# Attention block: 24 of 36 probability tiles turned through memory in the second batch, one fetch a tile, y kept in the order of rows 4 i + a

## The chip, the cores and the metric

One NeuronCore of a Trainium2 chip runs one program. Its engines are TensorE (PE, matmuls; its weight loads are PEld), VectorE (DVE), ScalarE (ACT), GpSimd (POOL) and SyncE (SP, which here only issues DMAs). ACT issues DMAs too, on a queue of its own. The metric is the device time of one execution in microseconds (us), the median of the runs; lower is better.

## The reference, cut to what matters

```python
x = x + attention(layernorm(x))        # x: 2 batches x 1024 rows x 512
x = x + lora_mixture(layernorm(x))

def attention(x):                      # 32 query heads, 8 key/value heads, head size 128
    q, k, v = x @ Wq.T, x @ Wk.T, x @ Wv.T          # split into heads
    q, k = rmsnorm(q) * q_norm_w, rmsnorm(k) * k_norm_w
    scores = q @ k.T / sqrt(128) + slope[head] * (column - row)     # causal
    return softmax(scores) @ v @ Wo.T

def lora_mixture(x):                   # 8 experts of rank 16
    gates = 8 * softmax(x @ Wr.T + br)
    return 2 * sum over experts of gates * ((x @ A.T) @ B.T)
```

All values are float32. Softmax, the products and both sums have to come out in float32 precision, so the kernel splits the operand of a large product into a high and a low part and multiplies three times.

## The kernel before

**Work and stages.** `attention_lora_block` goes through 16 groups, numbered w = 0 to 15. A group is one key/value head with its G = 4 query heads in one batch; w = 0 to 7 are the first batch, 8 to 15 the second. Within a group it goes through s = 0 to 7, the row tiles of P = 128 query rows. The first batch turns and splits the weights on the chip and keeps the results in memory (`keep_wkv`, `keep_wq`, `keep_wo`); the second batch loads them back (`back_wkv`, `back_wq`, `back_wo`). The second half of the block (the items that begin with `f_`, and `logits`, `lora`) runs for the first batch in groups 7 and 8 and for the second in group 15.

**One row tile.** `scores` multiplies q by k into `s_ps`. `score_max` (L989, item `max`) on DVE adds the bias, writes the scores into `probs` and finds the maximum; `exp` on ACT; `invert` on DVE; `normalise` (L876) on POOL multiplies a head's row by the inverse sum. `probs[s % 2]` then holds 128 rows of (s + 1) x 128 probabilities for four heads. `values` (L1233) needs them turned, a tile of 128 columns (number j, 0 to s) at a time, four heads side by side, 128 x 512. There are 36 such tiles in a group. They are turned in one of two ways:

- *By PE.* `turn` (L1115, `of == "p"`) makes four 128 x 128 transposes against `ident` into a bank of `turn_ps` (L1193). `high` on ACT makes `pT_hi` of it (L789), `low` on DVE makes `pT_lo` (L979).
- *Through memory*, for the tiles in `MEMORY_TILES` (one table each for w = 0 to 6, for w = 7 and for w = 8 to 15; 20, 16 and 20 tiles). `send_p` (L635) writes one head's tiles from `probs` into `p_bounce` when its `normalise` is done (waited for at L605), one DMA a head. `fetch_p` (L645) waits until the row tile's four sends have landed, and brings tile j back into `p_raw` so that the 32 x 32 blocks lie at their turned places: four DMAs, one for each 32 partitions. `flip_p` (L984) on DVE turns the 32 x 32 blocks in place (L987), `upper_p` (L793) on ACT makes `pT_hi` (L797), `lower_p` (L884) on POOL makes `pT_lo` (L887). The tables say for the tiles of a row tile which ones these are, and `values_order` puts them behind those turned by PE.

`values` adds up `o_ps` over the tiles, three matmuls each. `o_high` and `o_low` split it into `oT_hi` and `oT_lo`, `y` multiplies by Wo into `y_ps` with twelve matmuls, and `add_y` (L1032) adds it to `y`. `y` is a buffer of [128, 8, 512] that holds x first: `load_y` (L656) loads a tile of 128 rows with one DMA, partition p holding row p; in the first batch `x_stats` (L904) and `x_norm` take x from it, in the second from `w_raw`, where `load_x` (L662) puts it. `store` (L683) writes a tile of y to the output with one DMA.

```python
blocks = p_bounce[s % 2, j].rearrange("h (a i) (b j) -> b i (h a) j", i=BLOCK, j=BLOCK)
for b in range(NBLK):
    sp.dma_start(raw_p(n)[b * BLOCK:(b + 1) * BLOCK, :].rearrange("p (n j) -> p n j", j=BLOCK),
                 blocks[b]).then_inc(p_fetched[n], 16)
```

**What sets the order.** Six strings write it out by hand: `PROLOGUE` (w = -1), `GROUP_A` (w = 0 to 6), `BOUNDARY` (7), `FIRST_B` (8), `GROUP_B` (9 to 14) and `LAST` (15). Each engine's program is the items that it knows, in the order of the string (`follow`, L423); an item waits by semaphores for what it needs. So SP's one queue issues sends, fetches, the loads of y and x and the stores in the string's order, and an item that waits holds up all behind it on its engine. In `GROUP_B`, for instance, the fetch of tile 2 of row tile 7 stands behind that row tile's last send. The loads of weights, the keeps and the loads back are issued by ACT, but for the first ones, which SP issues (L619 to L633).

## Time and profile before

| | us |
|---|---|
| median of 3 runs | 2056.68 (2056.5 to 2058.53) |
| profiled execution, its own time | 2058.6 |
| its span, first to last instruction | 2056.5 |
| PE busy | 1993.2 |
| DVE, ACT, POOL busy | 1363.5, 1162.6, 1189.2 |

The profile records one execution. Its granted clock is 0.997 of full speed over the span. DMA packets: 896141, 283.81 MB; 677721 of them are under 512 B. An engine's busy time is the time that at least one of its instructions covers; PE's matmuls are pipelined and their ends are modelled, so their lengths overlap, and what one costs is better read from the starts. SP's rows (SPq) are DMA issues: the length is what the issue takes on the queue, and the landing comes later. Line numbers are those of the kernel before. The timeline joins instructions of one kind that follow each other (x4 for four). The middle groups of either batch repeat each other; a group's end is taken as the end of its last `add_y`.

### The profile page before, as it was taken

To read this page: it belongs to the slowest core of one execution; us is meant where nothing else is said; L and a number is where in the kernel's file an instruction comes from. 1 tells how busy PE (TensorE), PEld (TensorE's weight loads), DVE (VectorE), ACT (ScalarE), POOL (GpSimd) and SP (SyncE) were. 2 spreads that over 40 slices of the span, in tenths; PEclk is the share of its full clock that TensorE was granted. 3 is DMA by queue.
4 is the path that set the end of the run, shared out by engine and by line. 5 is a ranking of instruction groups with operands and counts; after the bars stand their busy time and mean duration, and the time that the engine had idled before them with its cause. 6 is when DMAs were issued, how large, how long until landed. Compare 5 with 4: busy or idle time off the path is not lost.

```text
span 2056.5 us, 33589 instructions
## 1 busy us (share of the span) xinstructions
PE 1993.2 (97%) x10956; PEld 1698.1 (83%) x10956; DVE 1363.5 (66%) x3431; ACT 1162.6 (57%) x3314; POOL 1189.2 (58%) x1188
## 2 busy tenths in 40 slices
PE   7999999999999999999999899999999999999996
PEld 6888888888888888888888788787878878788774
DVE  6667667666666666768876566565666656566696
ACT  4656656565665656655555465555656555465552
POOL 3574645647465574655645557465664746657473
PEclk9999999999999999999999999999999999999998
DMA  4573855657466573765635637365463745637254
GB/s 164 138 161 119 192 141 150 132 154 166 129 171 145 136 159 113 181 181 142 135 109 141 142 96 173 96 154 139 123 124 108 172 101 137 161 81 165 69 122 99
DMA packets 896141, 283.81 MB, mean 138 GB/s; under 512 B 677721, under 2 KB 839513, under 8 KB 895969
## 3 DMA queue, kind: packets, MB, share of 16 engines
q1 hardware_dynamic: 844064, 179.44, 41.7%
q10 hardware_dynamic: 51904, 102.24, 14.2%
q8 instruction: 88, 1.44, 0.3%
q14 instruction: 85, 0.69, 0.1%
HBM read 152.59 MB, written 128.97 MB: 137 GB/s over the span
## 4 chain that ended last, share of the span: by engine, by line
PE 76%; SPq 8%; DMA 4%; DVE 4%; issue 4%; POOL 2%; ACT 2%; DVEq 0%; POOLq 0%; ACTq 0%
PE s_ps L1106 16%; PE q_ps L1106 15%; PE y_ps L1106 14%; PE o_ps L1106 14%; PE turn_ps L1193 9%; SPq L653 7%; PE turn_ps L1106 7%; DMA p_bounce<-probs_odd 2%; POOL probs_odd L881 1%; DMA p_raw_b<-p_bounce 1%; DMA p_bounce<-probs_even 1%; DVE oT_lo L1029 1%; PE turn_ps L1187 1%; SPq L642 1%; ACT oT_hi L823 1%
## 5 line engine op out<-in xcount | busy, mean ns | idle before, releaser
L881 POOL TENSOR_TENSOR probs_odd<-probs_odd,p_inv 128x256 f32<-128x256 f32 (+3 forms) x256 | 318.0, 1257 | 180.1 <-DVE p_inv L1008 179.2
L881 POOL TENSOR_TENSOR probs_even<-probs_even,p_inv 128x128 f32<-128x128 f32 (+3 forms) x256 | 261.3, 1043 | 191.3 <-DVE p_inv L1008 190.5
L1106 PE MATMUL s_ps<-kT_hi,qT_hi 128*128 128x512 f32 (+3 forms) x768 | 272.5, 355 | 4.1 <-DVE neg_max L1001 3.8
L1001 DVE CUSTOM_DVE_ANT_0 probs_odd<-s_ps,rel 128x256 f32<-128x256 f32 (+3 forms) x256 | 209.3, 820 | 97.3 <-issue 96.6
L802 ACT ACTIVATE probs_odd<-probs_odd,neg_max 128x256 f32<-128x256 f32 (+3 forms) x256 | 212.2, 831 | 91.7 <-DVE neg_max L1001 91.6
L1106 PE MATMUL s_ps<-kT_hi,qT_lo 128*128 128x512 f32 (+3 forms) x768 | 262.4, 342 | 0.0
L1106 PE MATMUL s_ps<-kT_lo,qT_hi 128*128 128x512 f32 (+3 forms) x768 | 261.7, 341 | 0.0
L802 ACT ACTIVATE probs_even<-probs_even,neg_max 128x128 f32<-128x128 f32 (+3 forms) x256 | 185.1, 725 | 118.7 <-DVE neg_max L1001 118.4
L1001 DVE CUSTOM_DVE_ANT_0 probs_even<-s_ps,rel 128x128 f32<-128x128 f32 (+3 forms) x256 | 174.9, 687 | 109.8 <-issue 108.8
L987 DVE STREAM_TRANSPOSE p_raw<-p_raw 128x512 f32<-128x512 f32 x252 | 174.9, 700 | 83.5 <-DMA p_raw<-p_bounce 83.2
L1106 PE MATMUL q_ps<-wqT_hi,xnT_hi 128*128 128x512 f32 x512 | 217.2, 424 | 1.0 <-DVE qn L1012 0.8
L1106 PE MATMUL y_ps<-woT_hi,oT_hi 128*128 128x512 f32 x512 | 204.8, 400 | 10.9 <-DVE oT_lo L1029 8.6
L789 ACT ACTIVATE pT_hi<-turn_ps 128x512 fp32r<-128x512 f32 x260 | 154.3, 597 | 107.3 <-PE turn_ps L1193 107.3
L887 POOL TENSOR_TENSOR pT_lo<-p_raw,pT_hi 128x512 fp32r<-128x512 f32 x134 | 173.8, 1301 | 49.7 <-ACT pT_hi L797 49.6
L1106 PE MATMUL q_ps<-wqT_hi,xnT_lo 128*128 128x512 f32 x512 | 201.6, 394 | 0.0
L1106 PE MATMUL y_ps<-woT_hi,oT_lo 128*128 128x512 f32 x512 | 200.5, 392 | 0.0
L1106 PE MATMUL q_ps<-wqT_lo,xnT_hi 128*128 128x512 f32 x512 | 200.4, 391 | 0.0
L1106 PE MATMUL y_ps<-woT_lo,oT_hi 128*128 128x512 f32 x512 | 199.9, 390 | 0.0
L979 DVE TENSOR_TENSOR pT_lo<-turn_ps,pT_hi 128x512 fp32r<-128x512 f32 x260 | 174.8, 677 | 27.2 <-ACT pT_hi L789 26.1
L811 ACT ACTIVATE qn<-q_ps 128x128 f32<-128x128 f32 x512 | 134.7, 280 | 94.9 <-PE q_ps L1106 93.9
L1106 PE MATMUL o_ps<-pT_hi,v_hi 128*128 128x512 f32 x426 | 177.3, 416 | 4.5 <-DVE pT_lo L979 3.7
L1106 PEld LDWEIGHTS s_ps<-kT_hi,qT_hi 128*128 128x128 f32 x768 | 144.6, 188 | 32.0 <-DVE neg_max L1001 9.1
(131 smaller groups left out, 5068.3 us busy)
## 6 DMA issues: line engine op xcount, KB each, us to landing
p_raw<-p_bounce SPq DMA_DIRECT2D x1008, 64.0 KB, 2.3
p_bounce<-probs_odd SPq DMA_DIRECT2D x60, 384.0 KB, 3.1
p_raw_b<-p_bounce SPq DMA_DIRECT2D x256, 64.0 KB, 2.4
p_bounce<-probs_odd SPq DMA_DIRECT2D x60, 256.0 KB, 2.8
p_bounce<-probs_even SPq DMA_DIRECT2D x60, 256.0 KB, 3.0
p_bounce<-probs_even SPq DMA_DIRECT2D x64, 192.0 KB, 2.4
wq_kept<-wqT_hi ACTq DMA_DIRECT2D x8, 1024.0 KB, 4.5
wq_kept<-wqT_lo ACTq DMA_DIRECT2D x8, 1024.0 KB, 6.8
```

Source lines behind the costliest of these rows:

```text
L642: sp.dma_start(p_bounce[s % 2, first:s + 1, h].rearrange("u p c -> p u c"), probs[s % 2][:, h, first * P:(s + 1) * P].rearrange("p (u c) - ...
L653: sp.dma_start(raw_p(n)[b * BLOCK:(b + 1) * BLOCK, :].rearrange("p (n j) -> p n j", j=BLOCK), blocks[b]).then_inc(p_fetched[n], 16)
L789: nc.scalar.activation(target, bank, ACT.Copy).then_inc(sems["high"], 1)
L802: nc.scalar.activation(row, row, ACT.Exp, bias=neg_max[:, s % 2, h:h + 1], scale=-1.0, accum_out=p_sum[:, s % 2, h:h + 1]).then_inc(sems[" ...
L811: last = nc.scalar.activation(qn[:, h, :], q_ps[:, h * HD:(h + 1) * HD], ACT.Square, scale=float(slopes[gg % NG * G + h]), accum_out=q_sum ...
L881: nc.gpsimd.tensor_tensor(row, row, p_inv[:, s % 2, h:h + 1].to_broadcast((P, L)), ALU.mult).then_inc(sems["normalise"], 1)
L887: nc.gpsimd.tensor_tensor(p_low(r), raw_p(raw_tile[w, s, j]), p_high(r).bitcast(F32), ALU.subtract).then_inc(sems["lower_p"], 1)
L979: nc.vector.tensor_tensor(target, bank, upper.bitcast(F32), ALU.subtract).then_inc(sems["low"], 1)
L987: nc.vector.transpose(raw, raw).then_inc(sems["flip_p"], 1)
L1001: nc.vector.tensor_tensor_reduce(out=probs[s % 2][:, h, 0:L], in0=s_ps[:, at_col:at_col + L], in1=rel[:, S - L:S], scale=-float(slopes[w % ...
L1106: last = nc.tensor.matmul(target, a, m, start=start and i == 0 and k == 0, stop=stop and i == len(pairs) - 1 and k == 2)
L1193: last = nc.tensor.transpose(bank[0:width, i * rows:(i + 1) * rows], source, ident[0:rows, 0:rows])
```

## The change

`MEMORY_TILES` gives the groups of the second batch four more tiles through memory: tile 1 of row tiles 2, 3 and 7, and tile 2 of row tile 6. The first batch's tables stay as they are.

`p_bounce` gets another layout, [2, head, tile, block b of 32 columns, row, 32 columns]. A send now writes pieces of 32 columns (128 B), where it wrote 128 columns (512 B). A fetch reads, for partition b x 32 + i and each head, the rows 4 i to 4 i + 3 of block b in one piece (512 B), so that one DMA to 128 partitions brings the tile. After the flip, column a x 32 + i of a head holds row 4 i + a of the row tile. The turn of p by PE writes its columns in the same order (`rows_in_order`), so the values, `y_ps` and the buffer `y` have their rows in that order too: partition a x 32 + i holds row 4 i + a. `load_y` and `store` use four DMAs a tile for it, 32 partitions each; before the first group, two of the four are issued by SP and two by ACT. The turn of x in the first batch, whose x comes out of `y`, puts the rows back in order.

All six strings of the order are written anew: the same items, but for those of the four tiles a group that change their way. The core of the diff (of the strings, only the first line of `PROLOGUE` is shown):

```diff
@@ -23,280 +23,281 @@
 MEMORY_TILES = ({2: (2,), 3: (2, 3), 4: (2, 3, 4), 5: (2, 3, 4, 5), 6: (3, 4, 5, 6), 7: (2, 3, 4, 5, 6, 7)},
                 {2: (2,), 3: (2, 3), 4: (3, 4), 5: (3, 4, 5), 6: (4, 5, 6), 7: (3, 4, 5, 6, 7)},
-                {2: (2,), 3: (2, 3), 4: (2, 3, 4), 5: (2, 3, 4, 5), 6: (3, 4, 5, 6), 7: (2, 3, 4, 5, 6, 7)})
+                {2: (1, 2), 3: (1, 2, 3), 4: (2, 3, 4), 5: (2, 3, 4, 5), 6: (2, 3, 4, 5, 6), 7: (1, 2, 3, 4, 5, 6, 7)})
 PROLOGUE = (
-    "load_y.2 load_y.0 load_y.1 load_y.3 load_y.7 x_stats.2 load_y.4 x_stats.0 load_y.6 x_stats.1 load_wkv.first "
...
+    "load_y.0 load_y.3 load_y.1 load_y.2 load_wkv.first x_stats.0 x_moments.0 x_stats.3 x_rstd.0 load_wq.first "
...
 )
...
@@ -533,6 +534,10 @@
             return raws[n]
 
 
+        def rows_in_order(columns):
+            return columns.rearrange("p (a i) -> p i a", a=NBLK)
+
+
         early = [name for name in p_slot if name[0] < NG - 1]
         last_early_slots = [[name for name in early if p_slot[name] == TURN_SLOTS + MEMORY_SLOTS + i][-1] for i in range(MORE_SLOTS[0])]
         last_early_raws = [[name for name in raw_tile if name[0] < NG - 1 and raw_tile[name] == RAW_TILES + i][-1] for i in range(MORE_RAW[0])]
@@ -564,7 +569,7 @@
         def pairs(turned):
             return turned[:].rearrange("p (a c) n -> p a (c n)", c=2).bitcast(F32)
 
-        p_bounce = nc.dram_tensor("p_bounce", [2, NT, G, P, P], F32).ap()
+        p_bounce = nc.dram_tensor("p_bounce", [2, G, NT, NBLK, P, BLOCK], F32).ap()
 
         s_ps = psum("s_ps", [P, 1024])
         turn_ps = [psum(f"turn_ps{i}", [P, 512]) for i in range(RING)]
@@ -612,7 +617,8 @@
         @block.sync
         def _(sp):
             x_v = x.rearrange("b (t p) d -> b p t d", p=P)
-            out_v = out.rearrange("b (t p) d -> b p t d", p=P)
+            x_by_y = x.rearrange("b (t i a) d -> b t a i d", i=BLOCK, a=NBLK)
+            out_by_y = out.rearrange("b (t i a) d -> b t a i d", i=BLOCK, a=NBLK)
 
             def load_wkv(w, *first):
                 if first:
@@ -639,8 +645,8 @@
                 if before and h == 0:
                     after(sp, "flip_p", *before[0], through_memory(*before[0])[-1])
                 after(sp, "normalise", w, s, h)
-                sp.dma_start(p_bounce[s % 2, first:s + 1, h].rearrange("u p c -> p u c"),
-                             probs[s % 2][:, h, first * P:(s + 1) * P].rearrange("p (u c) -> p u c", c=P)).then_inc(p_sent[s % 2], 16)
+                sp.dma_start(p_bounce[s % 2, h, first:s + 1].rearrange("u b p j -> p (u b) j"),
+                             probs[s % 2][:, h, first * P:(s + 1) * P].rearrange("p (u j) -> p u j", j=BLOCK)).then_inc(p_sent[s % 2], 16)
 
             def fetch_p(w, s, j):
 
@@ -648,16 +654,16 @@
                 sp.wait_ge(p_sent[s % 2], sent[w, s])
                 if raw_before[w, s, j]:
                     after(sp, "lower_p", *raw_before[w, s, j])
-                blocks = p_bounce[s % 2, j].rearrange("h (a i) (b j) -> b i (h a) j", i=BLOCK, j=BLOCK)
-                for b in range(NBLK):
-                    sp.dma_start(raw_p(n)[b * BLOCK:(b + 1) * BLOCK, :].rearrange("p (n j) -> p n j", j=BLOCK),
-                                 blocks[b]).then_inc(p_fetched[n], 16)
+                tile = p_bounce[s % 2, :, j].rearrange("h b (i a) j -> (b i) h (a j)", a=NBLK)
+                sp.dma_start(raw_p(n).rearrange("p (h k) -> p h k", h=G), tile).then_inc(p_fetched[n], 16)
 
             def load_y(w, t):
                 b = 0 if w < 0 else 1
                 if b:
-                    sp.wait_ge(stored[t], 16)
-                sp.dma_start(y[:, t, :], x_v[b, :, t, :]).then_inc(y_loaded[t], 16)
+                    sp.wait_ge(stored[t], 16 * NBLK)
+
+                for a in range(NBLK if b else NBLK // 2):
+                    sp.dma_start(y[a * BLOCK:(a + 1) * BLOCK, t, :], x_by_y[b, t, a]).then_inc(y_loaded[t], 16)
 
             def load_x(w, t):
                 if t < 2:
@@ -683,15 +689,23 @@
             def store(w, t):
                 b = ffn_batch(w)
                 after(sp, "add_f", b, t)
-                sp.dma_start(out_v[b, :, t, :], y[:, t, :]).then_inc(stored[t], 16)
+                for a in range(NBLK):
+                    sp.dma_start(out_by_y[b, t, a], y[a * BLOCK:(a + 1) * BLOCK, t, :]).then_inc(stored[t], 16)
 
             for t in range(NT):
-                sp.wait_ge(stored[t], 16 * NB)
+                sp.wait_ge(stored[t], 16 * NBLK * NB)
 
         @block.scalar
         def _(act):
+
+            x_by_y = x.rearrange("b (t i a) d -> b t a i d", i=BLOCK, a=NBLK)
+
+            def load_y(w, t):
+                if w < 0:
+                    for a in range(NBLK // 2, NBLK):
+                        nc.scalar.dma_start(y[a * BLOCK:(a + 1) * BLOCK, t, :], x_by_y[0, t, a]).then_inc(y_loaded[t], 16)
 
             def load_wkv(w, *first):
                 if not first and w + 2 < NG:
@@ -832,7 +846,7 @@
                 after(act, "turn", "wr")
                 nc.scalar.activation(b_sorted.rearrange("p o h r -> p h o r"), b_raw, ACT.Copy).then_inc(sems["sort_b"], 1)
 
-            follow({"load_wkv": load_wkv,
...
+            follow({"load_y": load_y, "load_wkv": load_wkv, "load_wq": load_wq, "load_wo": load_wo, "keep_wkv": keep_wkv, "keep_wq": keep_wq,
 
@@ -903,7 +917,7 @@
 
             def x_stats(w, t):
                 b = ln_batch(w)
-                dve.wait_ge((x_loaded if b else y_loaded)[t], 16)
+                dve.wait_ge((x_loaded if b else y_loaded)[t], 16 if b else 16 * NBLK)
                 nc.vector.bn_stats(x_stat[:, t, :], x_source(b, t)).then_inc(sems["x_stats"], 1)
 
             def x_moments(w, t):
@@ -982,7 +996,7 @@
                                                    ALU.subtract).then_inc(sems["low"], 1)
 
             def flip_p(w, s, j):
-                dve.wait_ge(p_fetched[raw_tile[w, s, j]], 16 * NBLK * raw_uses[w, s, j])
+                dve.wait_ge(p_fetched[raw_tile[w, s, j]], 16 * raw_uses[w, s, j])
                 raw = raw_p(raw_tile[w, s, j])
                 nc.vector.transpose(raw, raw).then_inc(sems["flip_p"], 1)
 
@@ -1030,7 +1044,7 @@
                                         ALU.subtract).then_inc(sems["o_low"], 1)
 
             def add_y(w, s):
-                dve.wait_ge(y_loaded[s], 16 * (w // NG + 1))
+                dve.wait_ge(y_loaded[s], 16 * NBLK * (w // NG + 1))
                 after(dve, "y", w, s)
                 nc.vector.tensor_tensor(y[:, s, :], y_ps[:], y[:, s, :], ALU.add).then_inc(sems["add_y"], 1)
 
@@ -1190,7 +1204,16 @@
                     return
                 rows, width = sources[0].shape[0], sources[0].shape[1]
                 for i, source in enumerate(sources):
-                    last = nc.tensor.transpose(bank[0:width, i * rows:(i + 1) * rows], source, ident[0:rows, 0:rows])
+                    columns = bank[:, i * P:(i + 1) * P]
+                    if of == "p":
+                        last = nc.tensor.matmul(rows_in_order(columns), source,
+                                                ident[:].rearrange("p (i a) -> p i a", a=NBLK), is_transpose=True)
+                    elif of == "x" and ln_batch(w) == 0:
+
+                        last = nc.tensor.matmul(columns.rearrange("p (i a) -> p a i", a=NBLK), source,
+                                                ident[:].rearrange("p (a i) -> p a i", a=NBLK), is_transpose=True)
+                    else:
+                        last = nc.tensor.transpose(bank[0:width, i * rows:(i + 1) * rows], source, ident[0:rows, 0:rows])
                 last.then_inc(sems["turn"], 1)
 
             def q_part(w, n, c):
```

## Rows read from the trace of the kernel before

**Rows 1.** The page: its part 1, and a line of its part 6 (DMA issues).
```profile
PE 1993.2 (97%) x10956; PEld 1698.1 (83%) x10956; DVE 1363.5 (66%) x3431; ACT 1162.6 (57%) x3314; POOL 1189.2 (58%) x1188
...
p_raw<-p_bounce SPq DMA_DIRECT2D x1008, 64.0 KB, 2.3
```

**Rows 2.** Windows, first batch: busy us (instructions) by engine, granted clock, DMA share, GB/s.
```profile
412.50:536.20 123.70, 122.85 (x687) 105.80 (x686) 81.94 (x200) 74.36 (x210) 72.78 (x70) 1.00 0.60 149
```

**Rows 3.** Windows, second batch: two middle groups and the last.
```profile
1302.80:1424.20 121.40, 118.69 (x644) 101.41 (x644) 75.46 (x190) 68.90 (x199) 72.97 (x70) 1.00 0.55 131
...
1668.00:1790.60 122.60, 118.85 (x644) 101.39 (x644) 75.45 (x190) 68.91 (x199) 72.93 (x70) 1.00 0.55 129
...
1912.20:2041.90 129.70, 120.49 (x611) 95.40 (x611) 103.67 (x277) 64.64 (x177) 74.10 (x78) 1.00 0.49 112
```

**Rows 4.** Waits of PE over six groups of the second batch, 1180.6 to 1912.2.
```profile
PE o_ps L1106 <- POOL pT_lo_b L887: 9.0, 12, 1.8
PE turn_ps L1193 <- DVE qn L1012: 5.5, 6, 0.9
PE y_ps L1106 <- DVE oT_lo L1029: 4.0, 6, 1.5
```

**Rows 5.** Timeline of PE around one turn of a tile: start us, length us.
```profile
1402.37 0.40 PE L1106 MATMUL o_ps<-pT_hi_b,v_lo 128*128 128x512 f32 x1
1402.60 0.60 PE L1193 MATMUL turn_ps<-ident,probs_odd 128*128 128x128 f32 x4
1402.96 0.48 PE L1106 MATMUL o_ps<-pT_hi_b,v_hi 128*128 128x512 f32 x1
1403.27 0.39 PE L1106 MATMUL o_ps<-pT_lo_b,v_hi 128*128 128x512 f32 x1
```

**Rows 6.** Groups of instructions by form: total busy us, mean ns, idle before.
```profile
L987 DVE STREAM_TRANSPOSE p_raw<-p_raw 128x512 f32<-128x512 f32 x252 | 174.9, 700 | 83.5 <-DMA p_raw<-p_bounce 83.2
L979 DVE TENSOR_TENSOR pT_lo<-turn_ps,pT_hi 128x512 fp32r<-128x512 f32 x260 | 174.8, 677 | 27.2 <-ACT pT_hi L789 26.1
L887 POOL TENSOR_TENSOR pT_lo<-p_raw,pT_hi 128x512 fp32r<-128x512 f32 x134 | 173.8, 1301 | 49.7 <-ACT pT_hi L797 49.6
...
L881 POOL TENSOR_TENSOR probs_odd<-probs_odd,p_inv 128x1024 f32<-128x1024 f32 x64 | 121.0, 1902 | 31.2 <-DVE p_inv L1008 31.2
...
L1193 PE MATMUL turn_ps<-ident,probs_odd 128*128 128x128 f32 x552 | 82.1, 274 | 10.1 <-DVE probs_odd L917 10.1
```

**Rows 7.** Timeline of SP, row tile 7 of one group: start us, length us.
```profile
1759.40 2.56 SPq L653 DMA_DIRECT2D p_raw_b<-p_bounce  x4
1762.01 1.08 SPq L642 DMA_DIRECT2D p_bounce<-probs_odd  x2
1766.31 1.91 SPq L653 DMA_DIRECT2D p_raw_b<-p_bounce  x4
...
1775.52 4.15 SPq L653 DMA_DIRECT2D p_raw_b<-p_bounce  x8
```

**Rows 8.** Windows: one send alone, then fetches alone.
```profile
1993.60:1996.00 2.40, 2.34 (x14) 1.75 (x13) 2.40 (x5) 0.62 (x2) 2.29 (x3) 1.00 0.51 147
2019.00:2028.00 9.00, 7.69 (x41) 6.11 (x39) 7.89 (x19) 3.52 (x7) 4.68 (x6) 1.00 0.77 123
```

**Rows 9.** Timeline of SP, the end of the last group.
```profile
2011.42 0.36 SPq L642 DMA_DIRECT2D p_bounce<-probs_odd  x1
2016.07 1.92 SPq L653 DMA_DIRECT2D p_raw_b<-p_bounce  x4
...
2024.46 4.15 SPq L653 DMA_DIRECT2D p_raw_b<-p_bounce  x8
2038.03 16.33 SPq L686 DMA_DIRECT2D out<-y  x4
```

**Rows 10.** Timeline of all engines, the start.
```profile
0.74 3.23 SPq L660 DMA_DIRECT2D y<-in_L_attn_x  x7
...
10.10 1.09 PE L1193 MATMUL turn_ps<-ident,probs_odd 128*128 128x128 f32 x4 [10.10 <-DVE probs_odd L917]
```

More of the change, by code:

```diff
@@ L833, in sort_b @@
                 nc.scalar.activation(b_sorted.rearrange("p o h r -> p h o r"), b_raw, ACT.Copy).then_inc(sems["sort_b"], 1)
-            follow({"load_wkv": load_wkv, "load_wq": load_wq, "load_wo": load_wo, "keep_wkv": keep_wkv, "keep_wq": keep_wq,
+            follow({"load_y": load_y, "load_wkv": load_wkv, "load_wq": load_wq, "load_wo": load_wo, "keep_wkv": keep_wkv, "keep_wq": keep_wq,
                     "keep_wo": keep_wo, "back_wkv": back_wkv, "back_wq": back_wq, "back_wo": back_wo, "high": high, "upper_p": upper_p, "exp": exp, "square_q": square_q, "v_high": v_high,
```

523 rows, old and new, of tables (BOUNDARY, FIRST_B, GROUP_A, GROUP_B) are left out of this document.

## The prediction

> **What bounds the kernel now.** I began with the page's busy shares: TensorE (PE) is busy 97% of the span, no other compute engine over 66% [rows 1]. So the time is PE's own work plus its idle stretches, and the views of windows by group say where these are. A group of the first batch takes 123.7 us, with PE idle 0.9 of it [rows 2]. One of the second takes 121.4 to 122.6 us and has PE idle 2.7 to 3.8; the last takes 129.7 with 9.2 idle [rows 3]. GpSimd (POOL) is busy 73 us of each, and the DMA engines 0.49 to 0.60 of the time, so neither is near its limit as an average. The view of PE's waits over six groups of the second batch names three: 9.0 us for POOL's `pT_lo_b`, in 12 waits, which is two a group; 5.5 for `qn`; 4.0 for `oT_lo` [rows 4].
>
> The first of these leads to the queue of SyncE (SP). In its timeline the last row tile's fetches start at 1766.31, when the sends have landed, and two tiles take 4.15 us [rows 7]: a tile comes each 2.1 us, because it is four issues of about half a us. VectorE (DVE) and POOL behind it need only 0.70 and 1.30 us a tile [rows 6]. So SP's issues set the pace of the tiles that PE waits for at the end of a group. The same stands at the end of the kernel: the last send is issued at 2011.42, the first fetch at 2016.07 (the send took 4.6 us to land), the last fetch ends at 2028.6 [rows 9].
>
> **The change, part by part.** All sums are against the profiled execution, 2058.6 us, which has a span of 2056.5 and 2.1 us around it; the median of the runs, 2056.68, is 1.9 us lower, and I take the same difference off both kernels.
>
> *Four turns fewer in each of eight groups.* The row of PE's transposes gives a mean of 274 ns [rows 6], and 128 of them would be 35 us. But these lengths overlap. In the timeline a turn starts at 1402.60, the next matmul at 1402.96, the one after at 1403.27; a matmul alone has a pitch of 0.23 (1402.37 to 1402.60) [rows 5]. So the turn of a tile costs 0.67 less 0.23, 0.44 us of PE. 32 tiles by 0.44 is **14.1 us less**. For each of them ACT converts from another place, DVE flips (700 ns) where it subtracted (677), and POOL subtracts (1301) [rows 6]: per group DVE +0.1 us, POOL +5.2, from 73 to 78 us of some 120. The cover of POOL's part is its idle 40%; without it, it would cost up to 5.2 us a group.
>
> *One fetch a tile.* The four issues, 2.1 us, become one, about 0.5. The stretch with fetches alone shows 0.77 of the DMA time at 123 GB/s [rows 8]: 0.77 by 16 engines by 128 B over 123 GB/s is 12.8 ns for a packet of 128 B. The stretch of a send, with packets of 512 B, shows 0.51 at 147 GB/s, so 28.4 ns. A tile is now 512 packets of 512 B, 32 an engine, 0.91 us, where it was 2048 packets, 1.64 us. The last of six tiles landed 6 by 2.1 less 0.5 plus 2.3 (landing), 14.4 us after the first issue [rows 1, 7]; the last of seven now lands after 7 by 0.91 plus some 1.9, or 8.3. It comes **6.1 us sooner** after its sends. The Trainium skill (DMA: Bandwidth & Descriptors, Issuing engines are not separate DMA queues) holds that issue time is usually small beside the transfer itself. The rows speak against that here, 2.1 us of issue against 1.64 of transfer; by the rule, this part would give next to nothing and the sum would be some 6 us smaller.
>
> *Sends in pieces of 128 B.* The packets swap sides: a row tile 7 send was 768 of 512 B (48 an engine, 1.36 us) and is now 3584 of 128 B, 224 an engine. No row shows a 128 B packet written to memory. The nearest are the two above: 12.8 ns for this size in the other direction, 28.4 ns for the larger size in this one. I take 12.8, by size, and keep 28.4 as the bad end. It makes 2.87 us a send, 1.5 more. POOL's normalise sets one head each 1.90 us [rows 6], so four heads also queue up 3 by 0.97, 2.9 us: the last lands 4.4 us later. Against that, two sends waited for the fetches issued before them (1759.40 to 1761.96) and went together at 1762.01 [rows 7]; now some 1.5 us of that is free. Net, for the last tiles, 6.1 plus 1.5 less 4.4 is 3 us sooner; for the first tile of row tile 7 about 2 later, which the work in between should hide: its values stand several us of PE's work behind its fetch in the order. So the 9.0 us of waits in six groups [rows 4], 10.5 in seven, should shrink. Bounds: gone wholly (-10.5), or doubled (+10.5), as the order of all items is new. I take **-4**.
>
> *The end.* The same gain, 3 us; the last store is four issues, of which three, 1.3 us, come on top. The other stores, five times four issues, are 9 us of SP; they start at 2038.03 as before, where the last store stood 16 us later [rows 9], so they are hidden. Net **-2**, between -5 and +3.
>
> *The start.* SP had seven loads of y, 3.2 us, ahead of the first weights, and PE began at 10.10 [rows 10]. Now four tiles stand ahead, in 16 issues split between SP and ACT; SP's eight take about the same 3.5 us, but 1 MB instead of 1.75 lies ahead of the weights, some 2 us of DMA, and tile 0 is normed first. ACT's issues fall before PE's first turn, for which ACT waits anyway. **-1**, between -4 and +3.
>
> *Rows 4 i + a.* The turn of p writes its columns with a step of 32 elements. No row shows a strided write by PE. Nearest are its own transposes with plain columns, at 0.11 us each; I take no change. The bad end is twice that, a rival below. A step on the input side is not there: the identity's columns are read in their order. The x turns (8 tiles) go the same way. The values keep their columns in the new order up to y, at no cost. The first batch's tile count is unchanged, and its PE idles 0.9 us a group [rows 2], so I give it nothing.
>
> Sum: -14.1 -4 -2 -1 is -21, 2037.5 for the profiled execution; **2035.6 us for the median**.
>
> **Rivals.** What this kernel's measurement can tell from no change is 0.2%, 4 us.
>
> (a) *The turns go, the waits don't.* The sends' queue eats what the fetches gain. -14 or less: 2042 to 2049. For: 4.4 us later sends. Against: SP's freed time. It is a faster one.
>
> (b) *The waits take it all back.* Seven tiles through POOL at 1.30 are 9.1 us, and their values are 4.8 us of PE; with 4 more tiles a group on that path PE waits 2 us more a group, 14 to 16 in all: 2052 to 2059. For: `pT_lo_b` is the longest wait already. Against: POOL's idle share.
>
> (c) *Slow writes, the other side.* If a 128 B packet to memory costs as much as a 512 B one, a send takes 224 by 28.4, 6.4 us; four are 25 against POOL's 7.6, and the last lands some 18 later than now, the fetches giving back 6. SP stands at the fetch, DVE, ACT and POOL have nothing for PE: 8 us or more a group in the second batch, 2 in the first (192 packets an engine, 5.5 us), 80 in all, so about 2115. It decides where four sends outrun the fetches' gain and the slack, 224 p = 1.9 + 2, at p of some 17 ns a packet. The Trainium skill (DMA: Bandwidth & Descriptors, Specifications) has a rule for it: below 512 B a transfer is read, modified and written. The fetches' 12.8 ns into SBUF show nothing of such a step; no row shows it into memory.
>
> (d) *Strided turns at half pace.* 228 tiles of p and 8 of x, by 4, by 0.11 more: +103 us, about 2140. For: nothing but the lack of a row. Against: the transposes' pitch, 0.11 us for 128 columns, is already twice that of a matmul's columns (0.23 for 512), so the writes come slowly.
>
> **How the numbers follow.** Chances: the forecast 0.60, (a) 0.14, (b) 0.08, (c) 0.13, (d) 0.05. The point is the forecast's, 2035.6. Its own terms reach down to 2056.7 - 14.1 - 10.5 - 5, about 2027; below that I see nothing. Upward the range takes in (a) and (b), to 2058, and leaves (c) and (d) out. Faster by over 0.2%: forecast and (a), 0.74. Within: most of (b), 0.07. Slower: (c), (d) and a little of (b), 0.19.
>
> **What would show it.** Right: PE's transposes of p 912 instead of 1040, at the same pitch; middle groups of the second batch at 119 us or less and of the first at 123.7; fetch issues 348 instead of 1264, tiles at most 1.3 us apart at the end of a group; the wait of PE for `pT_lo_b` below 9 us. Wrong: sends that land over 7 us after issue in row tile 7 and SP waiting for them (c), a pitch of 0.2 us for the turns of p (d), groups of the first batch longer than 124 us (either), or middle groups of the second still at 121.5 with PE waiting for POOL (b).

## The result, and the profile after

The changed kernel takes 2076.45 us (median of 4 runs, 2072.53 to 2078.79), the kernel before 2057.61 beside it. The ratio is 1.0084, 95% interval 1.0071 to 1.0097: 19 us **slower**, outside the range of 2027 to 2058, where 21 us faster was forecast. The profiled execution took 2077.55 us, with a span of 2074.5.

From the page of the changed kernel, its part 1 and lines of part 6 (DMA issues: count, size, median us to landing); they answer to [rows 1]:

```profile
PE 1988.2 (96%) x10828; PEld 1696.3 (82%) x10828; DVE 1367.7 (66%) x3431; ACT 1157.7 (56%) x3314; POOL 1237.1 (60%) x1220
...
p_raw<-p_bounce SPq DMA_DIRECT2D x272, 256.0 KB, 3.3
...
p_bounce<-probs_odd SPq DMA_DIRECT2D x32, 448.0 KB, 6.3
```

PE has 128 instructions fewer, as it should, but only 5 us less work, and it idles 86 us where it idled 63. The windows by group say where, with the columns of [rows 2]: a group of the first batch, two middle groups of the second, the last group, a stretch of row tile 7, and 3.4 us within it.

```profile
415.40:539.00 123.60, 122.67 (x687) 105.75 (x686) 81.58 (x200) 73.59 (x210) 73.76 (x70) 1.00 0.63 149
1313.30:1436.40 123.10, 118.29 (x628) 100.99 (x628) 74.97 (x190) 68.95 (x199) 78.54 (x74) 0.99 0.68 146
1436.40:1557.80 121.40, 117.73 (x628) 101.24 (x628) 75.83 (x189) 68.96 (x199) 77.54 (x74) 0.99 0.68 148
1928.20:2058.50 130.30, 118.11 (x595) 94.90 (x595) 103.21 (x277) 64.38 (x177) 79.24 (x82) 0.99 0.61 121
1519.50:1536.60 17.10, 15.77 (x83) 13.16 (x81) 9.46 (x17) 8.99 (x24) 15.74 (x13) 1.00 1.12 185
1538.20:1541.60 3.40, 3.40 (x11) 2.81 (x10) 2.29 (x4) 1.17 (x2) 0.74 (x1) 0.50 0.99 270
```

The first batch stands at 123.6, as before [rows 2] (one of its groups took 124.5). The middle groups of the second take 121.4 to 125.4 us with four turns fewer (six groups: 736.8 us, before 731.6), at a mean clock of 0.97 to 1.00, where every one had 1.00 before [rows 3]. The group at the boundary and the first of the second batch are 3.2 and 3.9 us longer, the start (up to the end of the first group) 3.3, the tail behind the last group 1.4, the last group 0.5, the first batch 0.3 in six groups. With the 5.2 of the middle ones these add up to the 18 us between the spans.

The waits of PE over the same six groups, 1191.4 to 1928.2, answer to [rows 4]:

```profile
PE turn_ps L1216 <- issue: 13.6, 6, 3.4
PE o_ps L1120 <- DVE oT_lo L1043: 7.3, 4, 2.5
PE turn_ps L1216 <- DVE qn L1026: 5.5, 6, 0.9
PE s_ps L1120 <- DVE neg_max L1015: 2.8, 3, 1.8
```

The wait for `pT_lo_b`, 9.0 us before, has gone. In its place PE waits 23.7 us for three things that are not probability tiles at all: the normed k (the turn of `kv_raw`, put down to "issue", since the trace doesn't name its releaser), `oT_lo` and `neg_max`. All three are written by VectorE. Its timeline in the changed kernel, one group:

```profile
1529.45 0.71 DVE L1001 STREAM_TRANSPOSE p_raw<-p_raw 128x512 f32<-128x512 f32 x1 [1.01 <-DMA p_raw<-p_bounce]
1534.10 0.71 DVE L1001 STREAM_TRANSPOSE p_raw_b<-p_raw_b 128x512 f32<-128x512 f32 x1 [3.93 <-DMA p_raw_b<-p_bounce]
1534.73 0.65 DVE L1026 TENSOR_TENSOR qn<-q_ps,q_inv 128x512 f32<-128x512 f32 x1
1535.31 0.67 DVE L966 COPY kv_raw<-turn_ps 128x512 f32<-128x512 f32 x1
1536.02 1.88 DVE L1032 TENSOR_TENSOR kv_raw<-kv_raw,k_inv 128x1024 f32<-128x1024 f32 x1
```

A flip stands 3.93 us for its fetch, with `qn`, the copy of kv and the norm of k behind it on the queue. By the order of `GROUP_B` this is not one of the added tiles: it is tile 6.6, the last of row tile 6. Its flip waits 2.8 to 3.9 us in all six middle groups, where it waited 0 to 1.2 before. In the group from 1313.30 on, the flips of 7.1 and 7.2 then wait 1.79 and 1.41 us ahead of `oT_lo`, for which PE stands 2.49. PE's timeline right after shows the price, twice over (start us, length us):

```profile
1538.00 0.95 PE L1216 MATMUL turn_ps<-ident,kv_raw 128*128 128x128 f32 x4 [2.73 <-issue]
...
1540.45 0.63 PE L1120 MATMUL o_ps<-pT_lo_b,v_hi 128*128 128x512 f32 x1
1540.88 0.63 PE L1120 MATMUL o_ps<-pT_hi_b,v_lo 128*128 128x512 f32 x1
...
1541.66 0.40 PE L1120 MATMUL o_ps<-pT_lo,v_hi 128*128 128x512 f32 x1
1541.90 0.39 PE L1120 MATMUL o_ps<-pT_hi,v_lo 128*128 128x512 f32 x1
1542.13 0.60 PE L1216 MATMUL turn_ps<-ident,kv_raw 128*128 128x128 f32 x4
```

PE idles 2.73 us, and from 1538.2 to 1541.6 it runs at a granted clock of 0.50, which is 1.2 GHz: a matmul each 0.43 us (1540.45 to 1540.88) in place of 0.23 to 0.24. That is some 1.6 us more. Nine such stretches stand in this execution between 15.8 and 2040 us, each behind an idle of PE; before, there was none between 14.4 and 2045.4.

The queue of SP in that stretch, which answers to [rows 7]:

```profile
1524.20 2.50 SPq L658 DMA_DIRECT2D p_raw<-p_bounce  x1
1526.75 0.50 SPq L648 DMA_DIRECT2D p_bounce<-probs_odd  x1
1527.34 2.81 SPq L658 DMA_DIRECT2D p_raw_b<-p_bounce  x1
1530.20 0.50 SPq L648 DMA_DIRECT2D p_bounce<-probs_odd  x1
1536.64 0.36 SPq L658 DMA_DIRECT2D p_raw_b<-p_bounce  x1
```

An issue here is no longer short: single fetches hold SP for 2.50 and 2.81 us while the DMA share is 1.12. The one at 1527.34 is tile 6.6's. It stands between the third and the fourth send of row tile 7, and the flip that waits for it starts 6.8 us after the issue began. The last send leaves at 1530.20, and row tile 7's first fetch 6.4 us later, when that send has landed.

The start, which answers to [rows 10]:

```profile
7.26 1.09 PE L1213 MATMUL turn_ps<-ident,probs_odd 128*128 128x128 f32 x4 [7.26 <-DVE probs_odd L931]
...
15.18 3.45 PE L1216 MATMUL turn_ps<-ident,w_raw 128*128 128x128 f32 x16 [3.40 <-DMA w_raw<-in_L_attn_Wq]
```

### The profile page after: what moved, and what is told of

It reads as the page before. It is cut to its first block, busy times and chain, and to the rows that moved or that the text cites. A ratio compares the mean times of both kernels' runs of the same rounds, so it can differ in the third digit from the quotient of the medians.

```text
span 2074.5 us, 32609 instructions
## 1 busy us (share of the span) xinstructions
PE 1988.2 (96%) x10828; PEld 1696.3 (82%) x10828; DVE 1367.7 (66%) x3431; ACT 1157.7 (56%) x3314; POOL 1237.1 (60%) x1220
## 4 chain that ended last, share of the span: by engine, by line
PE 74%; DMA 7%; DVE 5%; issue 5%; POOL 5%; SPq 2%; ACT 1%; ACTq 0%; DVEq 0%; POOLq 0%
PE q_ps L1120 15%; PE s_ps L1120 15%; PE o_ps L1120 14%; PE y_ps L1120 14%; PE turn_ps L1120 6%; PE turn_ps L1216 5%; PE turn_ps L1209 4%; DMA p_bounce<-probs_odd 2%; POOL probs_odd L895 2%; DMA p_raw_b<-p_bounce 2%; DMA p_raw<-p_bounce 2%; SPq L658 1%; SPq L648 1%; DMA y<-in_L_attn_x 1%; POOL probs_even L895 1%
## 5 line engine op out<-in xcount | busy, mean ns | idle before, releaser
L1001 DVE STREAM_TRANSPOSE p_raw<-p_raw 128x512 f32<-128x512 f32 x272 | 188.5, 699 | 97.2 <-DMA p_raw<-p_bounce 95.9
L901 POOL TENSOR_TENSOR pT_lo<-p_raw,pT_hi 128x512 fp32r<-128x512 f32 x143 | 185.0, 1302 | 81.3 <-ACT pT_hi L811 79.4
L868 POOL TENSOR_TENSOR q_sum_eps<-q_sum,q_eps 128x4 f32<-128x4 f32 x128 | 26.2, 205 | 276.4 <-ACT qn L825 276.2
L803 ACT ACTIVATE pT_hi<-turn_ps 128x512 fp32r<-128x512 f32 x228 | 135.0, 596 | 82.1 <-PE turn_ps L1209 82.1
L1120 PE MATMUL o_ps<-pT_hi,v_hi 128*128 128x512 f32 x410 | 170.5, 416 | 10.2 <-DVE oT_lo L1043 9.6
```

The lines of the kernel that those rows point to most:

```text
L803: nc.scalar.activation(target, bank, ACT.Copy).then_inc(sems["high"], 1)
L868: nc.gpsimd.tensor_tensor(sum_eps, source, eps, ALU.add).then_inc(sum_eps_done, 1)
L901: nc.gpsimd.tensor_tensor(p_low(r), raw_p(raw_tile[w, s, j]), p_high(r).bitcast(F32), ALU.subtract).then_inc(sems["lower_p"], 1)
L1001: nc.vector.transpose(raw, raw).then_inc(sems["flip_p"], 1)
L1120: last = nc.tensor.matmul(target, a, m, start=start and i == 0 and k == 0, stop=stop and i == len(pairs) - 1 and k == 2)
```

## The experiments

All were timed beside the kernel before, whose median was 2056.1 to 2057.3 in the four series; the ratio is to it. "Old order" is the strings of before, "new order" those of the change.

**The two halves of the change.** First the data path of before with the tables and strings of the change, then the reverse.

```diff
# old_path_new_order
 from before.py, with MEMORY_TILES, PROLOGUE, GROUP_A, BOUNDARY,
 FIRST_B, GROUP_B and LAST of the change
# new_path_old_order
 the changed kernel, with these seven blocks of before.py (20 tiles a group)
```

> The data path of before (512 B sends, four fetches a tile, y in plain rows) with the changed tables and all six changed strings. Theory P (path): the sends in 128 B pieces are what is late (they land after 6 to 7 us in row tile 7, and the DMA engines are full in row tiles 6 and 7), so with short sends the waits go and the four turns fewer a group show: 2035 to 2048. Theory O (order): the new strings ask PE for the turns of k (turn.k.0) before DVE, behind its flips, has normed k, whatever the path; then it stays at 2068 or more. Here the fetches are again 2.1 us of SP a tile, so if the new order needs the short fetch, it is also above 2065, with PE waiting for pT_lo_b and not for k.

Measured: 2146.36 us, ratio 1.0434 (1.0415 to 1.0454). Groups of the first batch took 125 to 128 us, middle ones of the second 129 to 134. PE waited 18.9 us for the normed k, 17.5 for `neg_max` and 10.9 for `pT_lo_b` over six groups. The new order with the 24 tiles leans on the short fetches; on the path of before it is far worse.

> The changed data path with the tables and strings of before (20 tiles a group). Theory P: late sends hurt here too, 2065 or more, with PE waiting for p in the second batch. Theory O: the path by itself is harmless or helps a little through the short fetches, 2045 to 2060. The start is that of before with y in pieces, some 1 us either way.

Measured: 2048.42 us, ratio 0.9965 (0.9952 to 0.9978). The windows of its groups (as above) and its waits over six groups:

```profile
415.80:539.50 123.70, 122.85 (x687) 105.76 (x685) 81.19 (x199) 74.21 (x210) 73.81 (x70) 1.00 0.62 149
1303.22:1422.74 119.52, 118.18 (x644) 101.53 (x644) 74.84 (x189) 69.17 (x199) 72.91 (x70) 1.00 0.58 133
1422.74:1541.66 118.92, 118.00 (x644) 101.52 (x644) 74.86 (x190) 69.23 (x199) 72.93 (x70) 1.00 0.60 134
```

```profile
PE turn_ps L1215 <- DVE qn L1025: 5.5, 6, 0.9
PE y_ps L1119 <- DVE oT_lo L1042: 3.2, 4, 1.2
```

So the path by itself is a gain of 8 us. The six middle groups sum to 717.2 us, 14.4 less than before, and the `pT_lo_b` waits are gone; the start gives 3.5 back, the tail 1.4. What is left of the change, four tiles more a group and the new order, costs 28 us on this path.

**Two mends that failed.** From the trace of the change I took the k turn that waits, and the load on the DMA engines, for the causes.

```diff
# k_turned_later: GROUP_B
-"... fetch_p.7.4 turn.k.0 lower_p.6.6 ... values.6.6 turn.k.1 o_high.6 ... q.9.0 high.k.0 o_low.6 ..."
+ turn.k.0 and turn.k.1 just ahead of values.7.3, high.k.0 ahead of high.k.1
# rows_from_6: row tiles 6 and 7 go the way of before
+if in_rows(s):      # s >= 6
+    for b in range(NBLK):
+        sp.dma_start(raw_p(n)[b * BLOCK:(b + 1) * BLOCK, :]..., blocks[b])
```

> The changed kernel with one edit in GROUP_B: turn.k.0 and turn.k.1 stand just before values.7.3 and high.k.0 just before high.k.1. Theory O: the wait of PE at turn.k (14.8 us over six groups) goes, and with it the stretches of 3.4 us at half clock that follow it, 1.7 us each: 2052 to 2062. Theory P: what is late is the tiles of row tiles 6 and 7, so the wait moves to the values behind it: 2068 to 2076.

Measured: 2089.05 us, ratio 1.016 (1.0145 to 1.0175), above the range of either theory. The wait for k (13.6 us in the view of the change, not 14.8) goes, and a longer one for `oT_lo` takes its place; over six groups:

```profile
PE o_ps L1120 <- DVE oT_lo L1043: 23.0, 6, 4.7
```

> The changed kernel, but row tiles 6 and 7 go the old way (512 B sends, four fetches of 32 partitions a tile, plain rows for p, x and y of these two). Theory P: the full stretch of the DMA engines is gone, sends of row tile 7 land in 3 to 4 us, most of the loss is gone: 2040 to 2055. Theory O: still 2068 or more.

Measured: 2099.82 us, ratio 1.021 (1.019 to 1.023). The sends of row tile 7 land 3.4 us after issue and the fullest 17 us of the middle groups have a DMA share of 0.97 (1.14 in the change), yet it is 23 us slower than the change. Full DMA engines are not the cause by themselves. The flip of 6.6 still waits 1.4 to 3.7 us; that the four issues a tile, some 2 us of SP, make the rest is likely and was not separated.

**Tiles or order.** In the old order I then made more tiles memory tiles one or two at a time. A tile's `fetch_p`, `flip_p`, `upper_p`, `lower_p` and `values` go just ahead of those of the row tile's next memory tile (its values no earlier than its `lower_p`), its `turn`, `high` and `low` go out. All else stands.

```diff
# on new_path_old_order; FIRST_B, GROUP_B, LAST
-turn.p.s.j ... high.p.s.j ... low.p.s.j
+fetch_p.s.j fetch_p.s.(j+1) ... flip_p.s.j flip_p.s.(j+1) ... (upper_p, lower_p, values alike)
# old_order_24:        (s, j) = 2.1, 3.1, 6.2, 7.1
# old_order_22:        (s, j) = 2.1, 3.1
# old_order_late_two:  (s, j) = 6.2, 7.1
```

> The changed data path with the order of before, in which only the four further tiles of each second-batch group (2.1, 3.1, 6.2, 7.1) are made memory tiles: their fetch, flip, upper and lower stand just ahead of those of the next memory tile of the row tile, their values just ahead of its values, their turn, high and low are gone. 24 tiles a group as in the change; every other item stands where it stood. Theory O (the rewritten order of items is what costs, the four tiles are worth their turns): below the 2048.4 us of the changed path with the old order and 20 tiles; the full saving of turns (32 turns of 0.44 us = 14.1 us) would give 2034 us, I expect 2034 to 2046, groups 8 to 13 of 117.5 to 119 us, no stretch at half clock in the middle. Theory T (the four tiles themselves cost more in sends, fetches, flips and splits than their turns give back, whatever the order): 2052 us or more, second-batch groups of 120.5 us or more, PE waits of over 1 us and half-clock stretches behind them.

Measured: 2090.46 us, ratio 1.017 (1.0154 to 1.0186). Slower than the change's own order with the same tiles.

> As the run before it, but only the two early tiles, 2.1 and 3.1, are added (22 memory tiles a group), in a stretch where the DMA engines are at half load and no tile is waited for long. Theory O: 2048.4 minus up to 7 us (16 turns of 0.44 us), so 2041 to 2047. Theory T in its strong form (any further tile costs): 2050 or more. If this one is faster than 2048.4 and the late two are slower, the late tiles are the ones that do not pay.

Measured: **2044.38 us, ratio 0.9941 (0.9927 to 0.9955)**. Two early tiles pay.

> Only the two late tiles, 6.2 and 7.1, are added (22 memory tiles a group), in the stretch in which all sends of row tiles 6 and 7 and their fetches fall together (DMA share 0.77 before, 1.12 in the changed kernel). Theory O: 2041 to 2047. Theory T: 2052 or more, sends of row tile 7 landing 6 us after issue in place of 5.0, and new waits of PE at turn.k or values of row tile 7.

Measured: 2095.20 us, ratio 1.0183 (1.0164 to 1.0202). Two late tiles cost 47 us over the same kernel without them. The four together are at 2090: the whole loss is the late two. The expectation of `old_order_22` had named this case; theory T holds for the late ones alone.

**The start.** In the same series, on `new_path_old_order`:

```diff
# weights_sooner: PROLOGUE
-"load_y.2 load_y.0 load_y.1 load_y.3 load_y.7 x_stats.2 ... load_wkv.first ... load_wq.first"
+"load_y.2 load_y.0 load_y.1 load_wkv.first load_y.3 load_wq.first load_y.7 x_stats.2 ..."
```

> The changed data path with the order and the 20 tiles of before (2048.4 us), but the first loads of Wk, Wv and Wq are issued behind three of y's tiles and not behind five. In that kernel PE waits 0.81 us for Wv and 0.87 us for Wq, and its first group is 3.5 us longer than before's 164.9. If y's pieces ahead of the weights make the start: the start group at 165.5 to 167, the whole 2045 to 2047. If the start's length comes from the four pieces of the later tiles of y, which now land behind Wq: no change or up to 2 us worse.

Measured: 2053.59 us, ratio 0.9986 (0.9978 to 0.9995), 5 us worse than without the edit. PE's first turn comes at 19.30 us instead of 10.87. The trace shows why: on DVE the statistics of tiles 3 and 7 of y, whose loads are now issued behind those of weights, stand 3.73 and 5.58 us for them, until 10.53 and 16.80, and the norm of the first tile that PE turns is behind them. (The expectation counts wrongly: the weights stood behind seven tiles of y, and now Wk and Wv stand behind three and Wq behind four.)

**Which late tile, and why.** On the 22 tiles of `old_order_22`:

```diff
# order_22_and_6_2:  (s, j) = 2.1, 3.1, 6.2
# order_22_and_7_1:  (s, j) = 2.1, 3.1, 7.1
# tile_7_1_last: as order_22_and_7_1, but
-fetch_p.7.1 fetch_p.7.2 ... flip_p.7.1 flip_p.7.2 ... values.7.1 values.7.2 ...
+fetch_p.7.2 ... fetch_p.7.1 fetch_p.7.7 ... flip_p.7.1 flip_p.7.7 ... values.7.1 values.7.7
# flips_behind_o_low: as order_22_and_7_1, but GROUP_B (FIRST_B and LAST alike)
-... flip_p.7.1 flip_p.7.2 ... norm_k ... low.p.7.0 q.9.0 o_high.6 fetch_p.7.6 o_low.6 ...
+... norm_k ... low.p.7.0 q.9.0 o_high.6 fetch_p.7.6 o_low.6 flip_p.7.1 flip_p.7.2 ...
```

> The version of 2044.4 us (changed path, order of before, early tiles 2.1 and 3.1 added) with the late tile 6.2 alone added. The late two together cost some 47 us over the same order with 20 tiles (2095.2 against 2048.4), and in that run PE waited up to 5.3 us a group at the end of row tile 7. Theory L (it is row tile 7's first fetched tile: its flip waits on DVE for the sends of row tile 7, and DVE's work for PE queues behind it, while PE has lost a turned tile to bridge with): 6.2 is nearly free, 2040 to 2052. Theory S (the sends and fetches of row tiles 6 and 7 as a whole are over what SP and the DMA engines carry): 6.2 costs about half, 2060 to 2075.

Measured: 2056.92 us, ratio 1.0002 (0.9993 to 1.0012): tile 6.2 costs 12.5 us, more than I held "nearly free".

> The same with the late tile 7.1 alone. Theory L: most of the loss stands here, 2075 to 2095, with the first flip of row tile 7 waiting over 4 us on DVE and PE waiting behind it for o_low or turn.k. Theory S: about half of it, 2060 to 2075.

Measured: 2079.79 us, ratio 1.0105 (1.0088 to 1.0121): tile 7.1 costs 35 us. The two add to the 47 of the pair. Its VectorE timeline:

```profile
1404.51 0.68 DVE L1027 TENSOR_TENSOR qn<-q_ps,q_inv 128x512 f32<-128x512 f32 x1
1408.77 0.71 DVE L1002 STREAM_TRANSPOSE p_raw<-p_raw 128x512 f32<-128x512 f32 x1 [3.58 <-DMA p_raw<-p_bounce]
1409.65 0.71 DVE L1002 STREAM_TRANSPOSE p_raw_b<-p_raw_b 128x512 f32<-128x512 f32 x1 [0.17 <-DMA p_raw_b<-p_bounce]
1410.28 2.29 DVE L1033 TENSOR_TENSOR kv_raw<-kv_raw,k_inv 128x1024 f32<-128x1024 f32 x1
1412.49 0.68 DVE L994 TENSOR_TENSOR pT_lo<-turn_ps,pT_hi 128x512 fp32r<-128x512 f32 x1
1413.09 0.67 DVE L1044 TENSOR_TENSOR oT_lo<-o_ps,oT_hi 128x512 fp32r<-128x512 f32 x1
```

PE's timeline of the same stretch, and its waits over six groups:

```profile
1409.34 0.39 PE L1121 MATMUL q_ps<-wqT_hi,xnT_lo 128*128 128x512 f32 x1
1413.82 0.79 PE L1121 MATMUL y_ps<-woT_hi,oT_hi 128*128 128x512 f32 x1 [4.10 <-DVE oT_lo L1044]
1414.41 0.63 PE L1121 MATMUL y_ps<-woT_lo,oT_hi 128*128 128x512 f32 x1
```

```profile
PE y_ps L1121 <- DVE oT_lo L1044: 22.7, 6, 4.4
```

The picture is the change's with another flip and another victim: here the flip of 7.1 waits 3.58 us for row tile 7's first fetch, the norm of k, a `pT_lo` and `oT_lo` of row tile 6 are behind it, PE idles 4.10 us, and the clock is at half for 6.8 us from 1412.2. In `old_order_22` the flip of 7.2, which stands at this place, waits too (2.30 us in that group), and PE loses little there: it has one more turn to do, and sends a seventh smaller land sooner (5.0 us in place of 5.7 in the mean of the middle groups).

The length of the flip's wait alone does not set the price. With 6.2 instead of 7.1 the flip of 7.2 waits longer, 3.6 to 4.7 us in the middle groups against 3.2 to 3.9, and PE's waits for `oT_lo` come to 7.5 us over the six instead of 22.7. What differs is that PE still has the turn of 7.1 to do.

> As the run before, but the fetch, flip, split and values of 7.1 stand behind those of 7.6, just ahead of 7.7's, so that only its turn is missing and no item of row tile 7's first fetched tile is doubled. If the loss is where DVE stands at the first flip (order), it goes: below 2055. If it is that PE lacks the turned tile that bridged the way of row tile 7 through memory (latency), it stays: 2065 or more.

Measured: 2062.62 us, ratio 1.0028 (1.0019 to 1.0038). Half of 7.1's 35 us goes, half stays; the outcome lies between the two theories. The first flip of row tile 7, now 7.2's, still waits 3.2 to 4.1 us in the middle groups.

> As order_22_and_7_1 (2079.8 us), but on DVE the flips of 7.1 and 7.2 stand behind the item o_low.6 (with their upper and lower behind them), so that DVE writes oT_lo for PE before it waits for the fetch. In the run with 7.1 the flip waited 3.58 us for its fetch, oT_lo came behind it, and PE waited 4.1 us. If the order on DVE is the loss: the wait for oT_lo goes and the time falls to 2045 to 2060. If the way through memory is too long for the work that PE has left, the wait only moves to the values of row tile 7 (pT_lo or pT_lo_b): 2065 or more.

Measured: 2058.22 us, ratio 1.0006 (0.9997 to 1.0016). 21.6 of the 35 us go. A middle group and the waits of PE over six:

```profile
1429.66:1549.81 120.15, 118.39 (x632) 100.15 (x632) 75.67 (x189) 69.25 (x199) 77.24 (x73) 1.00 0.66 145
```

```profile
PE o_ps L1121 <- POOL pT_lo_b L902: 1.7, 6, 0.3
PE o_ps L1121 <- POOL pT_lo L902: 1.7, 6, 0.3
```

The wait for `oT_lo` is gone and the clock is full in all middle groups. So the order on DVE was most of the loss of tile 7.1 in this kernel. What stays, 14 us over 22 tiles, is spread: 0.7 to 2.1 us in five of the six middle groups, 6.7 in the first of the second batch, 2 in the last. In the group shown PE is busy 118.39 us, 1.0 more than in `old_order_22` (117.39), with one turn fewer; the rows do not say why. That part was not divided further.

**Is it the same in the change?** Its own order, with tiles 6.2 and 7.1 of the second batch turned by PE again:

```diff
# change_less_late_two: on the changed kernel; FIRST_B, GROUP_B, LAST
-fetch_p, flip_p, upper_p, lower_p of 6.2 and 7.1
+turn.p.6.2 behind values.6.0 and low.p.6.1, high.p.6.2, low.p.6.2, values.6.2
+turn.p.7.1 behind turn.p.7.0, high.p.7.1, low.p.7.1, values.7.1
# MEMORY_TILES[2]: 6: (3, 4, 5, 6), 7: (2, 3, 4, 5, 6, 7)
```

> The changed kernel (2076.5 us) with its own order and strings, in which only tiles 6.2 and 7.1 of the second batch are turned on PE again (their fetch, flip, upper and lower are gone, their turn, high and low stand behind those of 6.1 and 7.0): 22 memory tiles a group. If the late tiles are what costs in the changed kernel too: 2040 to 2055 us, no wait of PE for kv_raw, few stretches at half clock. If the rewritten order itself costs: it stays at 2065 or more, since the two turns come on top and the order is kept.

Measured: **2046.42 us, ratio 0.9944 (0.9925 to 0.9963)**, 30 us less than the change. A middle group and its waits over six:

```profile
1306.39:1425.40 119.01, 117.39 (x636) 100.84 (x636) 75.00 (x190) 68.60 (x199) 76.08 (x72) 1.00 0.64 142
```

```profile
PE o_ps L1120 <- DVE pT_lo L993: 5.1, 6, 1.9
PE s_ps L1120 <- DVE neg_max L1015: 1.2, 1, 1.2
```

No wait for `kv_raw` or `oT_lo`; the six groups sum to 716.8 us. The flip of 6.6 waits 1.6 to 2.1 us in five of them; in the sixth it waits 3.1, PE stands 1.88 us behind it, the clock falls to half, and the group takes 123.0 us. The fullest 17 us have a DMA share of 1.10, near the change's 1.14, so the load on the DMA engines alone does not make the loss. With 22 tiles the new order (0.9944) and the old one (0.9941) are the same within their intervals; with 24 the new one is 14 us faster (2076.5 against 2090.5). The two late tiles were not tried one by one in the new order, nor was the flip of 6.6 put behind k there: for the change itself that the two tiles cost the 30 us is shown, and the way they do is read from the traces.

**Early tiles in both batches.** Last, the rule was pushed further, in the old order.

```diff
# both_batches_22: old_order_22, and (s, j) = 2.1, 3.1 in GROUP_A too
# both_batches_23: and 4.1 in both batches
```

> The version of 2044.4 us with the early tiles 2.1 and 3.1 made memory tiles in the first batch's seven groups too. PE is busy for 122.85 of 123.70 us in such a group, so each of the 14 x 4 turned blocks' work (two turns of 0.44 us a group) should come off in full if nothing turns late: 2 x 0.44 x 7 = 6.2 us, 2038 us. If the first batch has another bound (DVE and POOL carry the weights' copies there) it is 2044 or more, with PE waits in place of the turns.

Measured: **2038.77 us, ratio 0.9906 (0.9892 to 0.9921)**, the fastest, 18.5 us below the kernel before. Of the 6.2 us expected for the first batch 5.6 came. A group of the first batch:

```profile
413.17:536.32 123.15, 122.25 (x679) 104.99 (x677) 81.11 (x199) 74.33 (x210) 76.23 (x72) 1.00 0.67 158
```

PE's busy time falls from 122.85 to 122.25 for two turns: 0.30 us a turn. In the middle groups of the second batch two turns took it from 118.0 or 118.2 (20 tiles) to 117.39 (22), 0.3 to 0.4 each.

> The fastest version so far (2038.8 us: early tiles 2.1 and 3.1 through memory in both batches) with tile 4.1 added in both, 23 memory tiles in a second-batch group. If early tiles pay: 14 turns fewer, 2038.8 minus up to 6 us, 2033 to 2037. If row tile 4's larger sends and fourth fetch collide with row tile 5's (sends of row tile 5 already land 6.2 us after issue): 2040 or more.

Measured: 2085.07 us, ratio 1.0139 (1.0122 to 1.0155). In the second batch tile 4.1 brings nothing and costs nothing (middle groups 118.5 to 119.6). In the first, each group is 6.6 us longer. Such a group's window, and VectorE's timeline in the one before it:

```profile
433.20:562.94 129.74, 124.32 (x675) 106.50 (x673) 81.00 (x200) 74.30 (x210) 77.46 (x73) 0.97 0.66 154
```

```profile
363.83 0.65 DVE L1027 TENSOR_TENSOR qn<-q_ps,q_inv 128x512 f32<-128x512 f32 x1
369.26 0.71 DVE L1002 STREAM_TRANSPOSE p_raw<-p_raw 128x512 f32<-128x512 f32 x1 [4.78 <-DMA p_raw<-p_bounce]
369.91 1.08 DVE L1016 CUSTOM_DVE_ANT_0 probs_even<-s_ps,rel 128x896 f32<-128x896 f32 x1
```

The flip of tile 4.4 stands 4.78 us, the score maximum of row tile 6 is behind it, PE waits 4.4 us for `neg_max`, until 371.06, and the clock is at half from 369.2 for 6.8 us. As in the change, it is not the added tile's own flip. It isn't how late in the group a tile stands that decides, but whether a flip has to wait with something of PE's behind it. The first batch has three raw tiles (the buffers of `p_raw`) where the second has five, and SP waits there up to 7.4 us for POOL to free one. Here row tile 4's sends have landed at 358.23, and SP issues 4.4's fetch at 366.31, just after a `pT_lo_a` of POOL ends at 366.23. No run gives the first batch more raw tiles.

## Why the prediction was wrong

**The step that failed is the first: four turns fewer, 14.1 us, with POOL's part as the only thing to be covered.** I priced a tile's move by the busy time of each engine and named POOL's idle 40% as the cover. I didn't ask what stands behind a flip on VectorE when its fetch comes late. A flip's 0.70 us is nothing; its wait is 2.8 to 3.9 us for tile 6.6 in the change and 3.2 to 3.9 for 7.1 in the old order, and while it stands, `kv_raw`, `oT_lo` or `neg_max` stand too. The prediction had the delay itself: the first tile of row tile 7 some 2 us later, "which the work in between should hide". It asked that only of PE's values. The flip stands on VectorE ahead of other things that PE needs sooner. And the last tile of row tile 6, which the prediction did not price, is late too: its fetch lands 5.5 to 6.7 us after its issue, against 4.5 to 5.9 without the late two. The four tiles are worth −4 us for the early two (2048.4 to 2044.4) and +30 for the late two in the new order (2046.4 to 2076.5), +47 in the old: some +26 where −14.1 was forecast, which is the whole error of 40 us.

**The turn itself was over-sized.** 0.44 us from starts in one place of the timeline; PE's busy time fell by 0.30 to 0.4 a turn. 32 turns are some 10 to 13 us, not 14.

**Rival (b)** had the right step, more tiles through memory and a wait of PE of 2 us more a group, at 0.08. Its place was wrong (POOL's `lower_p`; the wait for `pT_lo_b` vanished), and it missed that each wait is followed by slow matmuls, so its 2052 to 2059 was 17 us too low. By the rows: waits over six groups 23.7 us against 6.3 without the late two, 17.4 more, and five half-clock stretches against one, four more at 1.6, 6.4 us, less 3.6 of turns: 20, and the groups show 736.8 less 716.8, 20.

**Fetches and waits, −4.** Right in kind, under-sized. In the old order with 20 tiles the middle groups fell by 14.4 us in six, beyond my bound of −10.5: `pT_lo_b` gone (9.0 us), 0.8 of `oT_lo`, and some 0.6 us a group of PE's busy time, which no part of the sum had. The upper bound, "doubled, as the order of all items is new", had the wrong cause: at 22 tiles the order makes no difference, and at 24 the new one is the better.

**Sends.** The 128 B packet was taken at 12.8 ns. A window of the change with one send in it:

```profile
1843.90:1845.10 1.20, 1.20 (x7) 0.97 (x6) 1.20 (x4) 0.93 (x2) 0.26 (x1) 1.00 0.81 126
```

0.81 by 16 engines by 128 B over 126 GB/s is 13.2 ns. **Rival (c)**, 28.4 ns, is out. The Trainium skill (DMA: Bandwidth & Descriptors, Specifications) has transfers below 512 B read, modify and write; whether that takes place no run here can show, and the price that (c) gave it, that of a 512 B packet, is not there. One sign named for (c) came all the same: 8 of the 32 sends of row tile 7 landed more than 7 us after issue, the latest 9.0, and SP waited for them. What my sum lacked is that these sends run beside the fetches of row tile 6: a send of 448 KB lands 6.3 us after its issue (median), and the fetches between the sends hold SP for 2.5 to 3.9 us each.

**End and start.** −2 and −1 were forecast; the tail is 1.4 us longer and the start 3.3. At the start PE did begin sooner, 7.26 against 10.10, and then waited 3.40 us for Wq. I had counted the bytes ahead of the weights and called it a gain, and not the pieces of y issued behind them by two queues. Wq lands 9.7 us after its issue, where it took 8.0 before, and ten pieces of y land between 12.5 and 16.3, beside it; that they delay it is argued. The longer tail goes with the path: it is 15.2 to 16.0 us in the runs that have it and 14.6 and 15.0 in the two that don't. The four issues of a store are in it; I didn't take it apart further.

**Rows 4 i + a, 0.** Right: the turns of p take 274 and 272 ns a matmul by the groups view, as in [rows 6], so **rival (d)** is out. **First batch, 0:** right to 1 us.

Of the signs named, those for "right" that came: 128 instructions fewer, 348 fetch issues, the first batch at 123.6, no wait for `pT_lo_b`. The tiles at the end of a group come 0.7 to 2.2 us apart, not always within 1.3. The one that failed outright was the middle groups, 121.4 to 125.4 instead of 119, and its cause was on none of my lists.

## What to carry to other kernels

When work is moved from one engine to a longer way through others, look at the in-order queues it passes: an instruction that waits for a transfer costs what stands behind it, not what it takes, as soon as the bounding engine runs out of other work. It need not be an added one: more traffic can make an old one late. Put it behind the items that the bounding engine needs next, and first move the pieces whose data are back before their turn; measure them piece by piece, since the same edit gave −4 us for two tiles, +12.5 for a third and +35 for a fourth. An idle of PE costs more than its length where the clock falls behind it.

## What was not expected of the hardware

- The granted clock fell to 0.50 in or right behind waits of PE (2.73 and 4.10 us in the rows above; the shortest 1.80 us, in the change), for stretches of 3.4 or 6.8 us, in which matmuls came each 0.43 us instead of 0.23.
- An issue on SP's queue took 0.36 to 0.5 us in the rows where nothing held it, and 2.50 and 2.81 us for a single 256 KB fetch in a stretch where the DMA share was 1.12.
- Packets of 128 B written to memory took 13.2 ns, near the 12.8 of [rows 8] for packets of this size in the other direction; and a transpose whose output has a step of 32 elements took no longer than a plain one.
